# GRU products of four of six steps written as pairs of 64-row products, with three changes of order around them

## The chip, the cores and the metric

The kernel runs on one core of a Trainium2 chip. The metric is the device time of one execution in microseconds, median of three runs. Engines are called by the profile's names: PE multiplies matrices (PEld is its loading of weights), DVE does elementwise work, ACT activations, POOL further elementwise work, SP issues DMAs.

## The reference, cut to what matters

A decoder layer on x of 4 x 1024 tokens of 256 features: a gated recurrence with layer norms, then three rounds of slot attention over 64 context rows, ending each in a GRU, then a routed expert layer. The change lies in the middle part:

```python
for _ in range(3):
    sn = rmsnorm(slots, slot_norm_w)
    scores = einsum('bkd,bmd->bkm', sn @ Wq.T, k_proj) * 256 ** -0.5
    attn = softmax(scores, axis=-2)
    attn = attn / (sum(attn, axis=-1, keepdims=True) + 1e-6)
    updates = einsum('bkm,bmd->bkd', attn, v_proj)
    xr, xz, xn = split(updates @ wih.T + bih, 3)
    hr, hz, hn = split(slots @ whh.T + bhh, 3)
    r, z = sigmoid(xr + hr), sigmoid(xz + hz)
    n = tanh(xn + r * hn)
    slots = (1 - z) * n + z * slots
```

## The kernel before

Features lie on partitions and tokens on columns. Every round of attention treats the batches in two pairs, so there are six **steps** k = 0 to 5; steps 1 to 4 are one loop in the program of each engine, and they are the steps two to five of the change's name. A step has eight **units** q = 0 to 7: batch of the pair h = q // 4, half of its 1024 tokens j = (q // 2) % 2, half of the features c = q % 2. A unit is called (k, q); its number in a row is u = 8k + q.

A unit's products are those of `unit` (L1443). Weights and states are split in a high and a low part (`w_hh0`, `w_hh1`; `slots_hi`, `slots_lo`), so a hidden product of a gate is 2 halves of the features times 3 passes, 6 matmuls of 128 rows. The attention of a batch has 64 context rows: the tile `at` has its high part on one half of the partitions and its low part on the other, and the folded values (`v_ih_pair`: value projection times W_ih, high and low, each on both halves) are multiplied with it in 2 matmuls of 128 rows. The low half of the attention is thereby also multiplied with the low part of the values. A unit has 24 matmuls of 512 columns in this order: r (6 hidden, 2 of the attention), hn (6), xn (2), z (6 and 2). The banks of r and hn rotate among three, z has two, xn one, and the scores two.

The other engines follow unit by unit, each in its written order. ACT: `r_gate` (L762, sigmoid of r), `n_gate` (tanh), `z_gate`. DVE: `candidate` (L1856: `hidden_part` adds a bias to hn and multiplies by r, `input_part` adds xn), then `settle` (L1903: a multiplication, an addition, and after every second unit `high`, the cast to `slots_hi`). POOL: `difference` (L1014, state less candidate) between tanh and settling, `add_squares`, and `low` (for `slots_lo`).

The attention of step k+1 is made during step k. ACT squares the settled states of step k-1 (`squares`, L783), POOL adds them, PE takes means (`mean_squares`, L1341, inside unit 2), ACT makes roots (`rms`), PE the scores (`scores`, L1350, between units 2 and 3), DVE the maximum (`tops`), ACT `exponentials` after r of unit 4, DVE `weights`, PE `sums` in unit 5, ACT `normaliser` (L753: table load, Ln, Exp, table load) after r of unit 6, DVE `attention` (L1826) and `spread_attention` (L1832: a cast to `at`, and the remainder). `spread_attention(k+1, 0)` serves units (k+1, 0) to (k+1, 3), and the one for h = 1 follows in step k+1.

The matmuls wait for what frees their banks and for their inputs: r of a unit for `t_dve` (hn read two units before), hn for `r_act` (the sigmoid of the unit before), xn for `t2_dve` (`input_part` of the unit before), z for `z_act`, and the first attention product of each h for `at_lo`. The loop on PE reads:

```python
unit(k, 0)
unit(k, 1)
unit(k, 2, {"HN": lambda: mean_squares(k + 1)})
scores(k + 1)
unit(k, 3)
unit(k, 4)
unit(k, 5, {"XN": lambda: sums(k + 1)})
unit(k, 6)
```

## Time and profile before

| | |
|---|---|
| median of 3 runs (lowest to highest) | 550.38 us (549.33 to 550.53) |
| the profiled execution | 551.15 us |
| its span, from the first to the last instruction | 549.4 us |
| PE busy | 504.2 us (92%) |
| DVE, ACT, POOL busy | 435.6 (79%), 340.0 (62%), 240.8 us (44%) |
| matmuls of `unit` (L1459) | 1128, 34% of the chain that ended last |
| from unit (1, 0) to the end of unit (4, 6) | 204.9 to 409.9 us of the span |

The page's busy times are shares of the whole span. The steps that the change touches are read as stretches: the chain that ended last shows which engine sets the time there, the timeline shows in brackets how long an engine stood idle before an instruction and for whom.

### The profile page before, as it was taken

How to read it: one execution, taken by the hardware profiler on the slowest of the kernel's cores; microseconds unless marked ns; L12 is line 12 of the kernel's file. 1: busy time of each engine (PE TensorE's matmuls, PEld its weight loads, DVE VectorE, ACT ScalarE, POOL GpSimd, SP SyncE). 2: the span in 40 equal slices, each digit the busy share in tenths (PEclk: the TensorE clock that was granted, in tenths of full speed). 3: DMA queues.
4: the chain of work that ended last, by engine and by line, in shares of the span. 5: the costliest groups of instructions: out<-in, count | busy, mean ns of one | idle time of the engine just before them, and what ended most of it. 6: DMA issues, size and time to landing. Idle time of an engine off the chain costs nothing.

```text
span 549.4 us, 7254 instructions
## 1 busy us (share of the span) xinstructions
PE 504.2 (92%) x2154; PEld 362.0 (66%) x2154; DVE 435.6 (79%) x794; ACT 340.0 (62%) x600; POOL 240.8 (44%) x209
## 2 busy tenths in 40 slices
PE   6999996959779998899999999999999999979993
PEld 2466552725557686488858876886787788867672
DVE  2899999998799477999966986898579667868783
ACT  3656549784598484567456846766565676547443
POOL 0122030200123255655934674555435266647776
PEclk9999999878889999999999999999999999989997
DMA  8965395560521032000000000001011145255741
GB/s 292 315 211 78 105 164 147 138 136 1 76 78 61 17 78 78 0 2 0 2 1 0 1 0 1 1 2 62 24 68 40 39 171 204 88 165 164 223 148 65
DMA packets 34886, 47.32 MB, mean 86 GB/s; under 512 B 8062, under 2 KB 26623, under 8 KB 34561
## 3 DMA queue, kind: packets, MB, share of 16 engines
q1 hardware_dynamic: 27216, 34.25, 20.6%
q0 software_dynamic: 7632, 12.62, 9.4%
q8 instruction: 18, 0.29, 0.2%
q14 instruction: 20, 0.16, 0.1%
HBM read 25.70 MB, written 16.83 MB: 77 GB/s over the span
## 4 chain that ended last, share of the span: by engine, by line
PE 49%; issue 7%; DVE 6%; POOL 4%; ACT 3%; DMA 1%; SPq 1%; POOLq 0%; ACTq 0%; DVEq 0%
PE psum L1459 34%; PE psum L1552 6%; PE psum L1270 3%; PE psum L1523 2%; PE psum L1401 1%; PE psum L1347 1%; POOL gru L1022 1%; DVE gru L1874 1%; DMA gathered<-sorted_rows 1%; POOL sorted_rows L1052 1%; DVE gru L1847 1%; DVE gru L1854 1%; POOL slots_lo L1037 1%; PE psum L1359 1%; POOL out L1060 1%
## 5 line engine op out<-in xcount | busy, mean ns | idle before, releaser
L1459 PE MATMUL psum<-slots_hi,w_hh 128*128 128x512 f32 x560 | 180.1, 403 | 1.6 <-ACT gru L767 1.6
L1459 PEld LDWEIGHTS psum<-slots_hi,w_hh 128*128 128x128 f32 x560 | 104.0, 190 | 28.3 <-issue 4.2
L1022 POOL TENSOR_TENSOR gru<-slots_full,gru 128x512 f32<-128x512 f32 x43 | 65.8, 1529 | 108.2 <-ACT gru L773 108.1
L1459 PE MATMUL psum<-slots_lo,w_hh 128*128 128x512 f32 x280 | 111.6, 399 | 0.0
L1459 PE MATMUL psum<-at,v_ih_pair 128*128 128x512 f32 x288 | 92.4, 406 | 4.5 <-DVE at L1753 3.1
L773 ACT ACTIVATE gru<-gru,vec 128x512 f32<-128x512 f32 x48 | 34.6, 722 | 59.6 <-DVE gru L1854 59.5
L1459 PEld LDWEIGHTS psum<-at,v_ih_pair 128*128 128x128 f32 x288 | 54.2, 192 | 21.3 <-DVE at L1753 3.4
L1155 PE MATMUL psum<-early_hi,w_in 128*128 128x512 f32 x128 | 58.4, 616 | 5.0 <-DMA early_hi<-in_xT 5.0
L1847 DVE SCALAR_TENSOR_TENSOR gru<-psum,vec,gru 128x512 f32<-128x512 f32 x48 | 35.9, 748 | 32.9 <-PE psum L1459 26.8
L1459 PEld LDWEIGHTS psum<-slots_lo,w_hh 128*128 128x128 f32 x280 | 53.0, 189 | 12.7
L1874 DVE TENSOR_TENSOR gru<-gru 128x512 f32<-128x512 f32 x47 | 43.6, 929 | 8.6 <-POOL gru L1022 7.5
L1155 PEld LDWEIGHTS psum<-early_hi,w_in 128*128 128x128 f32 x128 | 25.2, 198 | 35.7 <-issue 34.3
L1037 POOL TENSOR_TENSOR slots_lo<-slots_full,slots_hi 128x512 fp32r<-128x512 f32 x32 | 47.1, 1472 | 0.6 <-DVE slots_hi L1900 0.6
L1876 DVE TENSOR_TENSOR slots_full<-gru 128x512 f32<-128x512 f32 x47 | 44.5, 947 | 1.6
L767 ACT ACTIVATE gru<-psum,brz 128x512 f32<-128x512 f32 x48 | 32.6, 679 | 21.2 <-PE psum L1459 21.2
L1552 PE MATMUL psum<-slots_full,w_tile 128*128 x156 | 43.3, 400 | 1.1 <-issue 0.4
L1060 POOL DMA_INDIRECT out<-out_tile,out_index x39 | 37.9, 972 | 12.6 <-issue 8.8
L1052 POOL DMA_INDIRECT sorted_rows<-row_block,dest x32 | 33.8, 1056 | 20.0 <-DVE dest L1962 8.6
L1031 POOL TENSOR_TENSOR ss_block<-sq_block 128x512 f32<-128x512 f32 x16 | 22.3, 1392 | 40.8 <-ACT sq_block L788 37.3
L1854 DVE TENSOR_TENSOR gru<-psum,gru 128x512 f32<-128x512 f32 x48 | 33.2, 692 | 6.5 <-PE psum L1459 5.0
L780 ACT ACTIVATE gru<-psum,brz 128x512 f32<-128x512 f32 x48 | 32.5, 677 | 0.9 <-PE psum L1459 0.6
L1552 PEld LDWEIGHTS psum<-slots_full,w_tile 128*128 128x128 f32 x156 | 26.5, 189 | 8.8 <-issue 5.4
(249 smaller groups left out, 855.0 us busy)
## 6 DMA issues: line engine op xcount, KB each, us to landing
gathered<-sorted_rows SPq DMA_DIRECT2D x39, 129.0 KB, 2.3
x_scratch<-slots_full SPq DMA_DIRECT2D x8, 512.0 KB, 3.0
x_block<-x_scratch SPq DMA_DIRECT2D x8, 512.0 KB, 3.9
early_hi<-in_xT SPq DMA_DIRECT2D x3, 1024.0 KB, 5.3
v_ih_pair<-value_part SPq DMA_DIRECT2D x32, 96.0 KB, 2.2
x_tm<-in_x SPq DMA_DIRECT2D x4, 512.0 KB, 6.9
x_tm<-ln_b POOLq DMA_DIRECT2D x4, 512.0 KB, 6.0
slots_full<-expert_plus SPq DMA_DIRECT2D x1, 2048.0 KB, 9.7
```

Of the source, the lines that this page charges most:

```text
L773: act.activation(X(u), X(u), ACT.Tanh, bias=col(c, V_BIH + 2)).then_inc(n_act, 1)
L1022: pool.tensor_tensor(DF(u), full[:, c, seq(k, h), blk(j)], X(u), ALU.subtract).then_inc(d_pool, 1)
L1037: last = pool.tensor_tensor(slots[1][:, c, b, blk(j)], full[:, c, b, blk(j)], slots[0][:, c, b, blk(j)].bitcast(F32), ALU.subtract)
L1052: pool.indirect_dma_start(rows[:], bass.IndirectOffsetOnAxis(dest[:, n:n + 1], 0), rowb[:, row_slot(n), :], None, bounds_check=E * REGION - 1,
L1060: pool.indirect_dma_start(out[:], bass.IndirectOffsetOnAxis(oidx[:, g % 4, t:t + 1], 0), og[:, i % (4 * TG), :], None, bounds_check=TOK - ...
L1155: last = pe.matmul(psum[:, bank + j, :], wi[:, k, at_col:at_col + P], xF[b % 2][:, k, cols_of(j)], start=k == 0, stop=k == C - 1)
L1459: last = pe.matmul(psum[:, bank, :], w, d, start=start and i == 0, stop=stop and i == len(pairs) - 1, skip_group_check=begun or late)
L1552: last = pe.matmul(expert_out(i), wT[:, i % TG, c, :], ew[:, c, bass.ds(off, D)], start=c == 0, stop=c == C - 1)
L1847: dve.scalar_tensor_tensor(out=X(u), in0=psum[:, hn_bank(u), :], scalar=col(c, V_BHH + 2), in1=X(u), op0=ALU.add, op1=ALU.mult).then_inc(t ...
L1854: dve.tensor_tensor(X(u), psum[:, XN_B, :], X(u), ALU.add).then_inc(t2_dve, 1)
L1874: dve.tensor_tensor(Z(u), Z(u), DF(u), ALU.mult).then_inc(e_dve, 1)
L1876: dve.tensor_tensor(full[:, c, seq(k, h), blk(j)], X(u), Z(u), ALU.add).then_inc(s_dve, 1)
```

## The change

**Pairs.** In the units from (1, 1) to (4, 6), 30 in all, `split_unit` takes the place of `unit`. Each matmul of 128 rows becomes one on rows 0 to 63 ("low") and one on rows 64 to 127 ("high"). Both add into the same bank, the high ones after the low ones of that bank are done (semaphore `low_rows`). `both` issues a low product of one gate next to a high product of another: r low with what is left of the unit before (xn high, z high), hn low with r high, z low with hn high. So hn's high part ends with the unit, and xn and z of a unit end some ten pairs into the next one.

**A product less.** Low attention times low values is left out: of a gate's 4 half products of the attention 3 are issued. The third needs the high attention on one given half of the partitions, so SP copies `at`'s high part (64 partitions by 1024 columns) to the other half, into `at_x` (in the program's rows `value_parts`), one DMA for each h of a step (`copy_attention`, which waits for both token halves). The first pair of unit (k, 1) waits for the copy of h = 0, unit (k, 4) for that of h = 1. A unit has 22 or 23 pairs in turn.

**Order.** `mean_squares`, `scores` and `sums` move to places inside units 2, 3 and 6, after nine or ten pairs (in step 1 `mean_squares` comes after 15). On ACT `r_gate` of units 1, 3, 5 and 7 goes ahead of `squares`. On DVE `attention` and `spread_attention` for h = 0 are cut by token halves (`first_of_pair`); the first half goes ahead of `settle(k, 5)`, the second behind `candidate(k, 7)`; `candidate`s of units 1 to 3 go ahead of `lows`, `second_of_pair` and `tops`. Semaphores are merged to make room for two new ones.

```diff
+                    low, high = both(one[0:2], x_before)
+                    if x_before:
+                        high.then_inc(xn_mm, 1)
+                        pe.wait_ge(low_rows, 4 * n_split - 4)
+                    low, high = both(one[2:], z_before[0:4])
...
+                        low, high = both(update(r, 0, lo, 1), z_before[4:6])
+                        low.then_inc(low_rows, 1)
+                        pe.wait_ge(r_act, u)
+                        low, high = both(two[0:max(nz - 6, 1)], z_before[6:])
...
+                        pe.wait_ge(low_rows, 4 * n_split - 3)
+                        n = len(two)
+                        low, high = both(two, r_hi[0:n])
+                        low.then_inc(low_rows, 1)
+                        highs = r_hi[n:]
...
+                    pe.wait_ge(t2_dve, u)
+                    low, high = both(update(XN_B, 2, lo, 0), highs[0:1])
...
+                    z_lo = hidden(z, 1, lo) + update(z, 1, lo, u % 2)
+                    n = len(highs)
+                    low, high = both(z_lo[0:n], highs)
...
+                        high.then_inc(r_mm, 1)
+                        pe.wait_ge(low_rows, 4 * n_split - 2)
+                        low, high = both(z_lo[n:], hn_hi)
+                        high.then_inc(hn_mm, 1)
...
+                    return update(XN_B, 2, hi, 1), hidden(z, 1, hi) + update(z, 1, hi, 1 - u % 2)
...
+                def copy_attention(k, h):
+
+                    n = 2 * k + h
+                    sp.wait_ge(at_hi, at_made(k, h, J - 1))
+                    if n > 2:
+                        sp.wait_ge(at_copied, 16 * (n - 2))
+                    if k > 1:
+                        sp.wait_ge(z_mm, U * (n - 1))
+                    sp.dma_start(at_x[half(1 - h), :].bitcast(F32),
+                                 at[n % 3][half(h), :].bitcast(F32)).then_inc(at_copied, 16)
...
+                    rest = split_unit(k, 1, rest)
+                    rest = split_unit(k, 2, rest, {"XN" if k == 1 else "R": lambda: mean_squares(k + 1)})
+                    rest = split_unit(k, 3, rest, {"R": lambda: scores(k + 1)})
+                    rest = split_unit(k, 4, rest)
+                    rest = split_unit(k, 5, rest)
+                    rest = split_unit(k, 6, rest, {"R": lambda: sums(k + 1)}, last=k + 2 == PAIRS)
```

The same on the engines. PE, the start of unit (1, 6) before: r takes 8 matmuls of 128 rows, then hn begins (L1459 is the one line of `unit`'s matmuls; the number is that of the buffer).

```order
L1459 MATMUL psum<-slots_hi,w_hh0 128x512 [waits t_dve]
L1459 MATMUL psum<-slots_hi,w_hh1 128x512
L1459 MATMUL psum<-slots_lo,w_hh0 128x512
L1459 MATMUL psum<-slots_hi,w_hh0 128x512
L1459 MATMUL psum<-slots_hi,w_hh1 128x512
L1459 MATMUL psum<-slots_lo,w_hh0 128x512
L1459 MATMUL psum<-at0,v_ih_pair1 128x512 x2
L1459 MATMUL psum<-slots_hi,w_hh0 128x512 [waits r_act]
L1459 MATMUL psum<-slots_hi,w_hh1 128x512
```

PE, the start of unit (1, 6) now: L1542 issues the low rows, L1545 the high rows, so r's low rows stand in turn with xn and z of unit (1, 5).

```order
L1542 MATMUL psum<-slots_hi,w_hh0 128x512 [waits low_rows,t_dve]
L1545 MATMUL psum<-at0,v_ih_pair1 128x512
L1542 MATMUL psum<-slots_hi,w_hh1 128x512
L1545 MATMUL psum<-at0,v_ih_pair1 128x512
L1542 MATMUL psum<-slots_lo,w_hh0 128x512 [waits low_rows]
L1545 MATMUL psum<-slots_hi,w_hh0 128x512
L1542 MATMUL psum<-slots_hi,w_hh0 128x512
L1545 MATMUL psum<-slots_hi,w_hh1 128x512
L1542 MATMUL psum<-slots_hi,w_hh1 128x512
L1545 MATMUL psum<-slots_lo,w_hh0 128x512
L1542 MATMUL psum<-slots_lo,w_hh0 128x512
L1545 MATMUL psum<-slots_hi,w_hh0 128x512
```

The 8 products of r are no longer a block of their own; two gates of the unit before end among them.

DVE before, from `candidate(3, 6)` on (L1847 and L1854; `settle` is L1874, L1876 and the cast L1900), with the attention for step 4 in L1828 to L1840:

```order
L1847 SCALAR_TENSOR_TENSOR gru<-psum,vec,gru 128x512
L1854 TENSOR_TENSOR gru<-psum,gru 128x512
L1874 TENSOR_TENSOR gru<-gru 128x512
L1876 TENSOR_TENSOR slots_full<-gru 128x512
L1900 CAST slots_hi<-slots_full 128x2x512
L1828 SCALAR_TENSOR_TENSOR sc<-sc,small,inv 128x1024
L1838 CAST at<-sc 64x1024
L1840 TENSOR_TENSOR at<-sc,at 64x1024
L1847 SCALAR_TENSOR_TENSOR gru<-psum,vec,gru 128x512
L1854 TENSOR_TENSOR gru<-psum,gru 128x512
```

DVE now, the same place in the program (`candidate` L2024 and L2031, `settle` L2051 to L2077, attention L1997 to L2010):

```order
L2024 SCALAR_TENSOR_TENSOR gru<-psum,vec,gru 128x512
L2031 TENSOR_TENSOR gru<-psum,gru 128x512
L1997 SCALAR_TENSOR_TENSOR sc<-sc,small,inv 128x512
L2008 CAST at<-sc 64x512
L2010 TENSOR_TENSOR at<-sc,at 64x512
L2051 TENSOR_TENSOR gru<-gru 128x512
L2053 TENSOR_TENSOR slots_full<-gru 128x512
L2077 CAST slots_hi<-slots_full 128x2x512
L2024 SCALAR_TENSOR_TENSOR gru<-psum,vec,gru 128x512
L2031 TENSOR_TENSOR gru<-psum,gru 128x512
L1997 SCALAR_TENSOR_TENSOR sc<-sc,small,inv 128x512
L2008 CAST at<-sc 64x512
```

The attention's first half of 512 columns moved ahead of `settle(3, 5)`, its second half behind `candidate(3, 7)`.

ACT before, in a step, from the normaliser's second table load on (L773 tanh and L780 z of unit 6, L788 squares, L767 r of unit 7):

```order
L760 ACT_TABLE_LOAD
L773 ACTIVATE gru<-gru,vec 128x512
L780 ACTIVATE gru<-psum,brz 128x512
L788 ACTIVATE sq_block<-slots_full 128x1024
L767 ACTIVATE gru<-psum,brz 128x512
L773 ACTIVATE gru<-gru,vec 128x512
```

ACT now, the same place (L801, L808, L795, L816):

```order
L788 ACT_TABLE_LOAD
L801 ACTIVATE gru<-gru,vec 128x512
L808 ACTIVATE gru<-psum,brz 128x512
L795 ACTIVATE gru<-psum,brz 128x512
L816 ACTIVATE sq_block<-slots_full 128x1024
L801 ACTIVATE gru<-gru,vec 128x512
```

r of unit 7 and the squares changed places.

## Rows read from the trace of the kernel before

**Rows 1.** Windows: stretch, us; busy us of PE, PEld, DVE, ACT, POOL; clock; DMA.

```profile
204.89:231.52 26.63, 23.00 (x97) 14.93 (x95) 22.38 (x24) 13.79 (x18) 15.38 (x14) 1.00 0.23 80
283.13:334.74 51.61, 51.52 (x222) 38.40 (x221) 41.40 (x47) 32.78 (x41) 29.52 (x21) 1.00 0.00 1
```

**Rows 2.** Chain that ended last, one step: start us, us, what.

```profile
299.23 27.44 PE psum L1459 x118
...
331.06 0.09 issue
```

**Rows 3.** Timeline, PE, step 1: start, us, instruction, idle before it and releaser.

```profile
219.70 0.74 PE L1459 MATMUL psum<-slots_hi,w_hh 128*128 128x512 f32 x2 [1.59 <-ACT gru L767]
...
221.58 1.94 PE L1347 MATMUL psum<-ss_block,mean_f 128*64 128x512 f32 x8 [0.21 <-POOL ss_block L1031]
...
227.94 3.65 PE L1270 MATMUL psum<-slots_full,fold 128*64 128x512 f32 x16 [1.83 <-ACT inv L742]
```

**Rows 4.** Timeline, ACT and DVE, the same place.

```profile
218.02 1.06 ACT L788 ACTIVATE sq_block<-slots_full 128x1024 f32<-128x1024 f32 x1 [3.44 <-DVE slots_full L1876]
...
218.64 3.44 DVE L1697 TENSOR_TENSOR slots_lo<-slots_full,slots_hi 128x512 fp32r<-128x512 f32 x2
```

**Rows 5.** Groups on PE by shape: count, busy us, mean ns, idle before.

```profile
L1155 PE MATMUL psum<-early_hi,w_in 128*128 128x512 f32 x128 | 58.4, 616 | 5.0 <-DMA early_hi<-in_xT 5.0
...
L1287 PE MATMUL psum<-stack_f,ones_halves 64*64 64x512 f32 x8 | 1.9, 602 | 0.0
```

**Rows 6.** Weight loads of three lines: ns min/median/max, first and last start, shape.

```profile
L1459 PEld LDWEIGHTS psum<-slots_hi,w_hh x560: 186/188/337, 148.2 to 478.3; 128*128 128x128 f32 x187
...
L1347 PEld LDWEIGHTS psum<-ss_block,mean_f x32: 132/136/137, 221.6 to 379.1; 128*64 128x64 f32 x32
...
L1287 PEld LDWEIGHTS psum<-stack_f,ones_halves x8: 129/133/133, 136.6 to 137.6; 64*64 64x64 f32 x8
```

**Rows 7.** Timeline, PE, from products of 128 columns to products of 64.

```profile
326.27 0.40 PE L1459 MATMUL psum<-slots_lo,w_hh 128*128 128x512 f32 x1
326.60 1.94 PE L1347 MATMUL psum<-ss_block,mean_f 128*64 128x512 f32 x8
```

**Rows 8.** Timeline, ACT, r of unit (3, 6) and the normaliser for step 4.

```profile
303.08 0.68 ACT L767 ACTIVATE gru<-psum,brz 128x512 f32<-128x512 f32 x1
...
306.22 1.06 ACT L759 ACTIVATE inv<-inv 128x1024 f32<-128x1024 f32 x1
307.31 1.28 ACT L760 ACT_TABLE_LOAD   x1
```

**Rows 9.** Timeline, DVE, settling, candidate and attention around the same place.

```profile
301.77 1.17 DVE L1874 TENSOR_TENSOR gru<-gru 128x512 f32<-128x512 f32 x1
302.97 1.67 DVE L1876 TENSOR_TENSOR slots_full<-gru 128x512 f32<-128x512 f32 x1
304.56 0.74 DVE L1847 SCALAR_TENSOR_TENSOR gru<-psum,vec,gru 128x512 f32<-128x512 f32 x1
305.34 0.69 DVE L1854 TENSOR_TENSOR gru<-psum,gru 128x512 f32<-128x512 f32 x1
305.94 0.68 DVE L1874 TENSOR_TENSOR gru<-gru 128x512 f32<-128x512 f32 x1
...
307.38 0.69 DVE L1900 CAST slots_hi<-slots_full 128x1024 fp32r<-128x1024 f32 x1
307.99 1.28 DVE L1828 SCALAR_TENSOR_TENSOR sc<-sc,small,inv 128x1024 f32<-128x1024 f32 x1
...
310.03 2.21 DVE L1840 TENSOR_TENSOR at<-sc,at 64x1024 fp32r<-64x1024 f32 x1
...
330.75 1.22 DVE L1840 TENSOR_TENSOR at<-sc,at 64x1024 fp32r<-64x1024 f32 x1
```

**Rows 10.** DMA issues: count, KB each, median us from issue to landing.

```profile
v_ih_pair<-value_part SPq DMA_DIRECT2D x32, 96.0 KB, 2.2
...
x_scratch<-slots_full SPq DMA_DIRECT2D x8, 512.0 KB, 3.0
```

More of the change, by code:

```diff
@@ L321, in block_of, with at_made @@
             return i // J, blk(i % J)
+        def at_made(k, h, j):
+            n = 2 * k + h
+            return n + 1 + n // 2 - (1 if k > 0 and h == 0 and j == 0 else 0)
         def pair_banks(t):
@@ L1506, in unit, with both @@
                     run(Z_B + u % 2, update(1), start=False).then_inc(z_mm, 1)
+                def both(lows, highs):
+                    low = high = None
+                    for i in range(max(len(lows), len(highs))):
+                        if i < len(lows):
+                            bank, w, d, start = lows[i]
+                            low = pe.matmul(psum[:, bank, :], w, d, start=start, stop=False, skip_group_check=True)
+                        if i < len(highs):
+                            bank, w, d, start = highs[i]
+                            high = pe.matmul(psum[:, bank, :], w, d, start=start, stop=True, skip_group_check=True)
+                    return low, high
@@ L1564, in _ @@
                 unit(0, 7)
+                rest = [], []
                 for k in range(1, LAST):
[L1566 to L1573 removed]
+                    if k == 1:
+                        unit(k, 0)
+                    else:
+                        rest = split_unit(k, 0, rest)
+                    rest = split_unit(k, 1, rest)
[4 more added lines that the diff above has]
+                    rest = split_unit(k, 6, rest, {"R": lambda: sums(k + 1)}, last=k + 2 == PAIRS)
                     if k + 2 < PAIRS:
[L1575 removed]
+                        rest = split_unit(k, 7, rest)
                 def tiles_after(*these):
@@ L2151, in _ @@
                 settle(0, 5)
-                attention(1)
-                spread_attention(1, 0)
+                first_of_pair(1, 0)
+                first_of_pair(1, 1)
                 candidate(0, 7)
```

195 lines of the change are left out of this document (149 added, 46 removed).

## The prediction

> **What bounds the kernel now.** I read the page's shares first, then the chain that ended last, then single steps. In the chain, from 231 us to 409 us every piece is PE's, but for a wait of 0.09 us a step [rows 2]. A step of 51.61 us has PE busy for 51.52, DVE for 41.40, ACT for 32.78 and POOL for 29.52, at a granted clock of 1.00, which is 2.4 GHz [rows 1]. So in steps 2 to 4 a product less on PE is time won, until another engine's chain becomes longer than PE's. 118 matmuls in a row took 27.44 us [rows 2]: one costs 0.2325 us, called a slot below. Step 1 is different: PE is busy for 23.00 of 26.63 us [rows 1] and stands idle three times, 1.59 us for a sigmoid, 0.21 for POOL's sums of squares, 1.83 for the roots [rows 3].
>
> **The slots.** 30 units of 24 matmuls are 720 slots. A split unit has 22 pairs (u even) or 23 (u odd). Counted in the program, units (1, 1) to (4, 6) have 675 slots with at least one half product, 18 of them with one alone (9 at the start, 9 at the end of the series), and 10 whole matmuls in unit (4, 6): 685. If a pair costs what a whole matmul costs, 35 slots go: 35 x 0.2325 = **8.1 us less**.
>
> That a pair costs a slot is no row of this trace; the nearest are products on a quarter of the array. Eight records of 64 rows by 64 columns took 1.9 us, 0.24 us each, where records of the full array and the same 512 columns took 58.4 / 128 = 0.456 us [rows 5]. Two ran at a time. They used other rows and other columns of the array; the new pairs share the columns. I take one slot, with 0.006 us either way: 4 pairs in 1.9 us are 0.475 us a pair against 0.456, of which a part is the ends of a short run. Where PE sets the time (685 less the 156 slots under the chain below) that is 3 us either way.
>
> The Trainium skill says in "TensorE: Matmul & The Clock Gate", LDWEIGHTS (loading the stationary operand), that a load of 32 rows takes as long as one of 128, because its time goes by columns. Two rows bear it out: 64 columns took 133 ns with 64 rows and 136 with 128 [rows 6]. By the page a pair then has two loads of full length, which speaks against the change; the sum above needs them to overlap, and the price of the other case is rival C.
>
> **Changes of form.** Where products of 128 columns give way to ones of 64, the next product started 0.33 us after the last, a slot and 0.10 [rows 7]. `mean_squares` and `scores` have such changes before and after. `sums` was of the same form as its neighbours and is now a whole product among pairs: two more a step, 4 x 2 x 0.10 = **0.8 us more**. Bounds: 0 and 1.6.
>
> **New waits of PE on itself.** High products wait for the low ones of their bank. A matmul takes 0.40 us from start to end [rows 7]; where only two slots (0.465) lie between the last low one and the first high one (units 0 and 4; in 2 and 6 other products stand between), about 0.08 is lost with the wake-up: 7 x 0.08 = **0.5 us more**, from 0 to 2.
>
> **Step 1.** r of unit (1, 1) was late because ACT had `squares` ahead of it and stood 3.44 us for DVE [rows 4]. With r ahead, the 1.59 goes. `scores` comes ten slots (2.3 us) into unit 3 instead of before it, which covers the 1.83. What is late next is xn of unit (1, 2): `candidate(1, 1)` can start on DVE only where the two `lows` of 3.44 us now start, at 218.6 [rows 4], and is done 1.5 us later [rows 9], while PE, with unit (1, 0) from 204.9 [rows 1] and so unit (1, 1) from 210.5, is there after 37 slots at 219.1. That keeps 1.2 with the wake-up, and the sums of squares some 0.3: of 3.63 us **2.1 less**. Bounds: 0.5 and 3.6.
>
> **Step boundaries: the copy.** This is the term that decides. In the old order `at` was ready a little before its first use. Now unit (k, 1) of steps 2, 3 and 4 starts with a wait for the copy of `at`, and that copy needs both token halves of the attention, the second of which stands behind `candidate(k-1, 7)`. The chain, from the end of r's products in unit 6:
>
> - product to its end 0.40 [rows 7], then sigmoid, table load, Ln, Exp: 303.08 to 307.28, 4.20 [rows 8]. Together 4.6.
> - DVE, first half: half of 1.28, of the cast of 0.69 and of the remainder of 1.22: 1.6. `settle(5)`: 0.68 twice and the cast of 0.69, 2.05. `candidate(7)`: 0.74 and 0.69. Second half to the cast: 1.0. With gaps of 0.2: 6.3 [rows 9]. Beside POOL's work the same operations took 1.17 and 1.67 instead of 0.68, and 2.21 instead of 1.22 [rows 9]; tanh of unit 6 comes 2.0 us after Exp (the second table load of 1.28 [rows 8] and itself), so POOL's difference falls on `settle(5)`. I add 0.5, by the first of these: 6.8. Were all of them stretched, it would be 9.8.
> - the DMA of 256 KB: between 2.2 (96 KB) and 3.0 (512 KB) [rows 10], say 2.5, and 0.2 for SP and PE to wake.
>
> That is 14.1 us. PE has work for 7 slots of unit 6, 23 of unit 7 and 22 of unit 0, 52 x 0.2325 = 12.1. PE waits 2.0 us, a part of it already in unit 0, where xn waits for `candidate(7)`. Three boundaries: **6.0 us more**. Bounds: all alone, DMA 2.2: 13.3, so 1.2 each, 3.6; all stretched, DMA 3.0: 17.6, so 5.5 each, 16.5. Behind the wait stands all of PE; SP has nothing else in its queue then, and the loads of x1 that follow its last copy wait for `mean_squares(5)` as before.
>
> The scores' wait of 0.09 a step, 0.3 in all, goes [rows 2]: from r's products in unit 2 to Ln's end ACT needs 0.4 and 3.1 us [rows 8], and PE has 17 slots, 4.0 us. The new order of `squares` leaves `mean_squares` about as much room as the boundary's delay takes from it: 0, at most 1 a step. The attention's halves cost DVE two instructions more a step, in gaps it has (10 us a step idle [rows 1]). After unit (4, 6) step 5 has whole units; it moves as it stands.
>
> **Sum.** -8.1 + 0.8 + 0.5 - 2.1 + 6.0 - 0.3 = -3.2 us. The profiled execution took 551.15 us, its span 549.4; the median of the runs is 0.8 under it. The difference goes against the median: 550.4 - 3.2 = **547.2 us**.
>
> **The rivals.**
> A. *The copy comes in time.* If the chain is no longer than 12.1 us, the boundaries cost nothing and the sum is -9.2: 541.2 us. For it: DVE idles a fifth of a step [rows 1], and the first half's operations can overlap in part, as 305.94 to 307.99 shows three operations in 2.05 us [rows 9]. Against: even without POOL beside it the rows add up to 13.3.
> B. *The copy takes PE's place* (slower). If the boundary costs more than 9.2 / 3 = 3.1 us, the gain is gone. At 4.5 each it is -9.2 + 13.5: 554.7 us. For it: remainder and settling have rows of twice the length [rows 9], and POOL's difference and sums fall there. Against: it takes more than four of these operations stretched, each time.
> C. *The halves don't run side by side* (slower). If the two loads of a pair follow each other, a slot is 2 x 0.188 [rows 6] = 0.376, 685 x 0.144 = 98 us more, and PE then covers the copy: about 640 us; if the products do, 685 x 0.2325 = 159 us more, about 700. For it: no row has two products on the same columns and other rows. Against: [rows 5]. The page's rule on loads gives this result only if loads queue, and eight loads of 0.133 fit into the 1.9 us of [rows 5] either way, so the trace doesn't decide it.
>
> **How the numbers follow.** Forecast (boundary 1.2 to 3.1, about 544 to 550) 0.45; A 0.22; B 0.26; C 0.07. A measurement of this kernel tells 0.2% (1.1 us) from no change. Faster by more than that: 0.36 of the forecast and A, 0.58. Within: 0.06 of the forecast and 0.05 of B, 0.11. Slower: 0.03 of the forecast, 0.21 of B, and C, 0.31. The range runs from A's time to B's with boundaries of 4.9: 541 to 556. It leaves out C, the longest boundaries, and A with a cheaper pair.
>
> **What would show it.** Right: pairs start 0.23 us apart at a clock of 1.00; step 2 takes about 51 us, of which PE idles some 2 us, in units 0 and 1, for DVE and for the copy; in step 1 no wait for `r_act`. Wrong in the slot: half products 0.19 us or more apart, in turn. Wrong at the boundary: no idle time before the first pair of unit (k, 1), or more than 3 us. Wrong elsewhere: PE waiting for `ssum_done`, for scores' roots or for `t2_dve` in the middle of a step.

## The result and the profile after

| | before | after |
|---|---|---|
| median (lowest to highest), four runs each, side by side | 550.45 us (549.33 to 550.91) | 562.02 us (560.28 to 562.62) |
| ratio of the two, 95% interval | | 1.021 (1.019 to 1.023) |
| span of the profiled execution | 549.4 us | 560.5 us |
| a step (from the scores of step 2 to those of step 3) | 51.61 us | 53.32 us |

The change made the kernel 2.1% slower; 547.2 was forecast, and the time lies outside the range of 541 to 556. The page after, PE, DVE and the granted clock in 40 slices:

```profile
PE 502.4 (90%) x2776; PEld 359.3 (64%) x2776; DVE 448.0 (80%) x809; ACT 341.7 (61%) x600; POOL 241.2 (43%) x209
...
PEclk9999999969889999999899999999998999989997
...
PE 37%; issue 11%; DVE 9%; POOL 7%; ACT 5%; DMA 1%; SPq 1%; POOLq 0%; DVEq 0%; ACTq 0%
```

The last line is the chain that ended last: PE has 37% of it, where it had 49%. In the steps DVE, ACT, POOL and "issue" (time for which the profile names no releaser) now have links in it, where before there was PE alone [rows 2]. The stretches from scores to scores, columns as in [rows 1]:

```profile
232.04:285.98 53.94, 51.37 (x390) 38.42 (x388) 47.47 (x55) 34.02 (x42) 31.59 (x22) 0.97 0.07 11
286.02:339.34 53.32, 49.92 (x391) 36.49 (x389) 45.03 (x50) 33.12 (x40) 29.81 (x21) 1.00 0.05 11
339.34:392.70 53.36, 49.97 (x392) 36.64 (x390) 44.34 (x49) 33.13 (x40) 29.84 (x21) 1.00 0.11 31
```

PE is busy for 1.6 us less a step than before (49.9 against 51.52), so the products did become cheaper; it is idle for 3.4 where it was idle for 0.1. One start of pairs, PE and its weight loads (start us, us, instruction):

```profile
296.23 0.39 PE L1545 MATMUL psum<-at,v_ih_pair 64*128 64x512 f32 x1
296.23 0.62 PE L1542 MATMUL psum<-slots_hi,w_hh 64*128 64x512 f32 x2
296.46 0.39 PE L1545 MATMUL psum<-at,v_ih_pair 64*128 64x512 f32 x1
...
296.23 0.18 PEld L1545 LDWEIGHTS psum<-at,v_ih_pair 64*128 64x128 f32 x1
296.23 0.18 PEld L1542 LDWEIGHTS psum<-slots_hi,w_hh 64*128 64x128 f32 x1
```

Low and high product start together, the next pair 0.23 us later, and both loads run at once. PE's waits around the boundary to step 3 and at the start of step 5 (in brackets the idle time before, and who ended it):

```profile
315.77 0.50 PE L1542 MATMUL psum<-at,v_ih_pair 64*128 64x512 f32 x1 [0.69 <-DVE gru L2031]
319.79 0.47 PE L1542 MATMUL psum<-slots_hi,w_hh 64*128 64x512 f32 x1 [1.90 <-issue]
328.34 1.94 PE L1375 MATMUL psum<-ss_block,mean_f 128*64 128x512 f32 x8 [0.81 <-POOL ss_block L1059]
...
420.75 1.21 PE L1429 MATMUL psum<-eye_and_gate,slots_full 128*128 128x137 f32 x8 [0.67 <-DVE eye_and_gate L2089]
429.74 0.71 PE L1429 MATMUL psum<-eye_and_gate,slots_full 128*128 128x137 f32 x4 [4.05 <-ACT row_block L824]
```

The first is xn of unit (3, 0), the second the first pair of unit (3, 1), which waits for the copy, the third `mean_squares` in unit (3, 2). The last two are the routing's tiles in unit (5, 0). (By this count the unit of [rows 8] is (2, 6), the sixth unit before the boundary to step 3. The text ahead of the prediction numbers it, and the normaliser with it, one step too high; nothing in the sums hangs on that.)

What led to the three waits is one chain over four engines. ACT, DVE and POOL, from r of unit (2, 6) on (L795 sigmoid, L787 the normaliser's Exp, L1997 and L2008 attention, L2051 and L2053 settling, L2031 end of a candidate, L1050 POOL's difference, L1059 its sum of squares; rows between them are left out):

```profile
305.01 0.68 ACT L795 ACTIVATE gru<-psum,brz 128x512 f32<-128x512 f32 x1
308.15 1.06 ACT L787 ACTIVATE inv<-inv 128x1024 f32<-128x1024 f32 x1
309.25 0.75 DVE L1997 SCALAR_TENSOR_TENSOR sc<-sc,small,inv 128x512 f32<-128x512 f32 x1 [1.28 <-ACT inv L787]
311.33 1.73 POOL L1050 TENSOR_TENSOR gru<-slots_full,gru 128x512 f32<-128x512 f32 x1 [2.53 <-ACT gru L801]
311.94 1.67 DVE L2053 TENSOR_TENSOR slots_full<-gru 128x512 f32<-128x512 f32 x1
315.03 0.69 DVE L2031 TENSOR_TENSOR gru<-psum,gru 128x512 f32<-128x512 f32 x1
316.41 0.42 DVE L2008 CAST at<-sc 64x512 fp32r<-64x512 f32 x1
317.63 1.76 POOL L1059 TENSOR_TENSOR ss_block<-sq_block 128x512 f32<-128x512 f32 x1 [4.57 <-DVE at L2010]
322.38 1.76 DVE L2051 TENSOR_TENSOR gru<-gru 128x512 f32<-128x512 f32 x1 [1.05 <-POOL gru L1050]
327.01 1.27 POOL L1059 TENSOR_TENSOR ss_block<-sq_block 128x512 f32<-128x512 f32 x1 [1.72 <-ACT sq_block L816]
```

From the sigmoid at 305.01 to `mean_squares` at 328.34 it took 23.3 us. Before, the same two points lay 303.08 [rows 8] and 326.60 [rows 7], 23.5 us apart, and PE worked all of that time. After, PE has 23.3 less its waits there, 19.5 us of work. The chain was there before the change too, but out of sight. POOL's last sum of squares ahead of `mean_squares` in the kernel before:

```profile
321.00 1.69 POOL L1031 TENSOR_TENSOR ss_block<-sq_block 128x512 f32<-128x512 f32 x1
```

It ended 19.6 us after the sigmoid of r, 3.9 us before PE came to `mean_squares`; after the change it ends 23.3 us after the sigmoid, and PE waits for it. This is the reading that the experiments test:

**Theory C.** A step is a closed loop of two parts: from `mean_squares` to r of unit 6, PE's work alone (30.0 us after, 28.1 before), and from r of unit 6 to the next `mean_squares`, the longer of PE's work and a chain over ACT, DVE and POOL. In pair units PE's work in the second part became 4.0 us shorter; the chain did not (it is 3.7 us longer). **Rivals**: each wait is a cost of its own, and the copy the main one (A); the new order on DVE is the cause (D), not the pairs.

### The profile page after: what moved, and what is told of

Its sections match the earlier page's. It is cut to its first block, busy times and chain, and to the rows that moved or that the text cites. A ratio compares the mean times of both kernels' runs of the same rounds, so it can differ in the third digit from the quotient of the medians.

```text
span 560.5 us, 8564 instructions
## 1 busy us (share of the span) xinstructions
PE 502.4 (90%) x2776; PEld 359.3 (64%) x2776; DVE 448.0 (80%) x809; ACT 341.7 (61%) x600; POOL 241.2 (43%) x209
## 4 chain that ended last, share of the span: by engine, by line
PE 37%; issue 11%; DVE 9%; POOL 7%; ACT 5%; DMA 1%; SPq 1%; POOLq 0%; DVEq 0%; ACTq 0%
PE psum L1542 10%; PE psum L1487 7%; PE psum L1718 6%; PE psum L1545 5%; PE psum L1298 3%; POOL gru L1050 2%; POOL slots_lo L1065 2%; PE psum L1429 2%; PE psum L1689 1%; POOL ss_block L1059 1%; PE psum L1375 1%; DVE gru L2024 1%; DVE gru L2031 1%; DVE slots_full L2053 1%; DVE at L2008 1%
## 5 line engine op out<-in xcount | busy, mean ns | idle before, releaser
L1542 PE MATMUL psum<-slots_hi,w_hh 64*128 64x512 f32 x356 | 115.1, 400 | 5.7 <-issue 5.7
L1545 PE MATMUL psum<-slots_hi,w_hh 64*128 64x512 f32 x356 | 114.4, 401 | 0.0
L1050 POOL TENSOR_TENSOR gru<-slots_full,gru 128x512 f32<-128x512 f32 x43 | 64.0, 1488 | 94.0 <-ACT gru L801 94.0
L1542 PEld LDWEIGHTS psum<-slots_hi,w_hh 64*128 64x128 f32 x356 | 66.0, 186 | 21.6 <-issue 12.0
L1542 PE MATMUL psum<-slots_lo,w_hh 64*128 64x512 f32 x178 | 70.9, 398 | 0.0
L1545 PE MATMUL psum<-slots_lo,w_hh 64*128 64x512 f32 x178 | 70.8, 398 | 0.0
L801 ACT ACTIVATE gru<-gru,vec 128x512 f32<-128x512 f32 x48 | 34.7, 723 | 54.8 <-DVE gru L2031 54.7
L1545 PEld LDWEIGHTS psum<-slots_hi,w_hh 64*128 64x128 f32 x356 | 64.7, 186 | 5.2
L1487 PE MATMUL psum<-slots_hi,w_hh 128*128 128x512 f32 x200 | 67.0, 417 | 0.0
L2024 DVE SCALAR_TENSOR_TENSOR gru<-psum,vec,gru 128x512 f32<-128x512 f32 x48 | 35.8, 745 | 29.6 <-PE psum L1545 18.5
L2053 DVE TENSOR_TENSOR slots_full<-gru 128x512 f32<-128x512 f32 x47 | 53.0, 1128 | 1.6
L795 ACT ACTIVATE gru<-psum,brz 128x512 f32<-128x512 f32 x48 | 32.8, 683 | 34.7 <-PE psum L1545 26.2
L2051 DVE TENSOR_TENSOR gru<-gru 128x512 f32<-128x512 f32 x47 | 45.5, 968 | 9.7 <-POOL gru L1050 8.6
L1065 POOL TENSOR_TENSOR slots_lo<-slots_full,slots_hi 128x512 fp32r<-128x512 f32 x32 | 49.0, 1532 | 0.6 <-DVE slots_hi L2077 0.6
L1059 POOL TENSOR_TENSOR ss_block<-sq_block 128x512 f32<-128x512 f32 x16 | 22.0, 1377 | 62.4 <-ACT sq_block L816 48.7
L1542 PE MATMUL psum<-at,v_ih_pair 64*128 64x512 f32 x111 | 40.8, 401 | 3.1 <-DVE gru L2031 3.1
L1487 PEld LDWEIGHTS psum<-slots_hi,w_hh 128*128 128x128 f32 x200 | 37.3, 196 | 8.1 <-issue 1.0
```

Of the source, the lines that this page charges most:

```text
L801: act.activation(X(u), X(u), ACT.Tanh, bias=col(c, V_BIH + 2)).then_inc(n_act, 1)
L1050: pool.tensor_tensor(DF(u), full[:, c, seq(k, h), blk(j)], X(u), ALU.subtract).then_inc(d_pool, 1)
L1065: last = pool.tensor_tensor(slots[1][:, c, b, blk(j)], full[:, c, b, blk(j)], slots[0][:, c, b, blk(j)].bitcast(F32), ALU.subtract)
L1487: last = pe.matmul(psum[:, bank, :], w, d, start=start and i == 0, stop=stop and i == len(pairs) - 1, skip_group_check=begun or late)
L1542: low = pe.matmul(psum[:, bank, :], w, d, start=start, stop=False, skip_group_check=True)
L1545: high = pe.matmul(psum[:, bank, :], w, d, start=start, stop=True, skip_group_check=True)
```

## The experiments

Times are medians, with the ratio to runs of the kernel before on the same chip. The first expectations call theory C "B", and those on what the pairs do to the room in it "W".

### The copy in halves

```diff
-                    sp.wait_ge(at_hi, at_made(k, h, J - 1))
+                    for j in range(J if h == 0 else 1):
+                        sp.wait_ge(at_hi, at_made(k, h, j if h == 0 else J - 1))
...
-                    if q == 1:
-                        pe.wait_ge(at_copied, 16 * (2 * k + h - 1))
+                    if q == 1 or q == J + 1:
+                        pe.wait_ge(at_copied, 16 * copied(k, 0, j))
...
```

> The copy of the attention for h = 0 goes in two DMAs, one per token half; the first pair of unit (k, 1) waits for the first half alone, and unit (k, 3) for the second. Theory A (the copy is a wait of its own): the wait of 1.9 us before unit (k, 1) goes three times, with the restart some 6 us in all, 562.0 - 5.7 to 6.2 = about 556 us. Theory B (one chain bounds the boundary: second half of the attention, POOL's sums, difference and settling of unit 7, squares, sums of squares, mean_squares): the wait before unit (k, 1) goes too, but PE then waits some 2 us more for ss_block in unit (k, 2); the time stays within 1 us of 562, or 1.4 us less if the stretch at half clock after the copy of step 2 does not come back.

Measured: 565.49 us, ratio 1.026 (1.023 to 1.030), slower than the change. PE's wait for `mean_squares`, and the clock (column after POOL) behind it:

```profile
328.32 3.50 PE L1381 MATMUL psum<-ss_block,mean_f 128*64 128x512 f32 x8 [2.46 <-POOL ss_block L1065]
...
328.30:331.70 3.40, 3.38 (x8) 0.77 (x8) 3.34 (x3) 0.98 (x2) 3.40 (x3) 0.53 0.00 0
```

The copy's wait went, and `mean_squares` of step 3 started at 328.32, where it had started at 328.34. Theory A falls: 1.9 us taken from one wait came back in the next. The time is 2.5 us above what theory C (there B) allowed, and that is the clock: after this wait it was granted at half for some 3 us, and the eight products took 3.50 us in place of 1.94. This came at all three boundaries; in the change it came at one.

### POOL's wait, alone and with the copy in halves

```diff
-                        pool.wait_ge(at_lo, at_made(k + 1, 0, J - 1))
+                        pool.wait_ge(at_lo, at_made(k + 1, 0, 0))
```

> POOL's third sum of squares of a step waits for the first half of the attention alone, not for the second; everything else is as in the changed kernel. Theory B: POOL is free some 3 us earlier for the difference of unit 7, settling and the sums of squares are earlier, and the wait of 0.8 us before mean_squares goes in steps 3 and 4 while the copy's wait of 1.9 stays: about 560.4 us. Against it: POOL then runs beside candidate(k, 7) and the second half on DVE and stretches them by up to 1 us each; then the copy's wait grows to 3 or 4 us, and the time is 562 to 567.

> Both edits: the copy in halves and POOL's wait on the first half alone. Theory A (waits that add up): what the two single edits gave, added. Theory B (one chain behind two waits): more than the sum of the two, since the copy in halves alone only moves the wait to mean_squares: 562.0 - 3 x 2.05 (copy) - 2 x 0.8 (sums of squares) = about 554.5 us, if POOL does not stretch DVE's work.

Measured: 568.36 us, 1.032 (1.027 to 1.036), and 565.78 us, 1.027 (1.024 to 1.031). First PE and DVE with POOL's wait alone, then PE with both edits:

```profile
322.23 0.76 PE L1542 MATMUL psum<-slots_hi,w_hh 64*128 64x512 f32 x1 [3.13 <-issue]
...
317.86 1.40 DVE L2008 CAST at<-sc 64x512 fp32r<-64x512 f32 x1
319.30 1.64 DVE L2010 TENSOR_TENSOR at<-sc,at 64x512 fp32r<-64x512 f32 x1
```

```profile
323.70 0.50 PE L1548 MATMUL psum<-at,v_ih_pair 64*128 64x512 f32 x1 [2.48 <-DVE gru L2037]
```

POOL's sums now ran beside the second half of the attention and stretched its cast from 0.42 to 1.40 us and the remainder from 0.69 to 1.64; the copy's wait grew to 3.1. With both edits neither the copy nor the sums of squares were waited for, and the wait stood at xn of unit (3, 1), for `candidate(3, 0)`. Alone, the edit is slower than either forecast for it. The forecast of 554.5 for the pair of edits missed: I had taken the links out that PE named and left DVE's row of work as long as it was, or longer. In both runs PE also ran at half clock behind the wait at all three boundaries (0.50 from 324.6 to 327.8 us with both edits).

### Settling ahead of the attention

```diff
                     candidate(k, 6)
-                    first_of_pair(k + 1, 0)
                     settle(k, 5)
+                    first_of_pair(k + 1, 0)
```

> On DVE settle(k, 5) goes back ahead of the first half of the attention, as it stood before the change; nothing else. DVE stands idle 1.3 us there for the normaliser, and settling takes 2 to 3 us. Theory (the boundary hangs on DVE's chain after the normaliser): that chain is 1.3 to 2.2 us shorter, so xn's wait of 0.7 in unit 0 goes and the copy's wait shrinks by what is left, each boundary gives 1.3 to 2.0 and step 5 as much: 562.0 - 4 x 1.7 = about 555 us. Rival (settle(k, 5) is stretched by POOL beside it and ends no earlier than the attention could start): within 1 us of 562.

Measured: 558.56 us, 1.016 (1.013 to 1.019). Settling fills DVE's idle time; r to `mean_squares` is 22.8 us instead of 23.3, a step 52.8. The direction is the theory's, the size half of it: half of what settling took ahead of the attention pushed the attention back (it starts 5.7 us after r instead of 4.2). By the profile the boundary to step 2 gave 3.0 us, 1.6 of them the half clock that did not come there, the other two 0.5 each, and the start of step 5, for which as much was expected, nothing: PE's wait for `row_block` is 4.11 us. The profiled execution was the fastest of this kernel, 2.1 us below the median.

### The new orders with whole products

PE's loop is that of the kernel before, the copy is left out, and ACT, DVE and POOL keep the orders of the change.

```diff
-                    rest = split_unit(k, 1, rest)
-                    rest = split_unit(k, 2, rest, {"XN" if k == 1 else "R": lambda: mean_squares(k + 1)})
-                    rest = split_unit(k, 3, rest, {"R": lambda: scores(k + 1)})
...
+                    unit(k, 1)
+                    unit(k, 2, {"HN": lambda: mean_squares(k + 1)})
+                    scores(k + 1)
+                    unit(k, 3)
...
```

> The changed kernel's orders on DVE, ACT and POOL, but whole products of 128 rows on PE in the old order of units, without the copy. Theory W (a pair unit leaves the other engines less room: hn's and xn's high rows end with the unit or two pairs into the next one, and the next xn comes ten pairs in, so that DVE has some 2 us for a candidate where whole units left it over 5): with whole units the new orders cost nothing at the boundaries; steps take 51.6 us with no wait in units 0 to 2, step 1 gains its 2 us, and only the start of step 5 stays late by some 4: 550.4 - 2 + 4 = about 552.5 us. Rival D (the new order of DVE makes the boundary late by itself): waits of 2 to 3 us stay at each boundary, 558 us or more.

Measured: 557.08 us, 1.013 (1.010 to 1.015). A step by the windows, POOL's last sum of squares in it, and PE's wait in step 5:

```profile
281.76:333.36 51.60, 51.51 (x222) 38.40 (x220) 44.69 (x51) 32.62 (x41) 30.90 (x20) 1.00 0.00 1
...
324.24 1.29 POOL L1041 TENSOR_TENSOR ss_block<-sq_block 128x512 f32<-128x512 f32 x1 [1.72 <-ACT sq_block L798]
...
423.54 1.25 PE L1411 MATMUL psum<-eye_and_gate,slots_full 128*128 128x137 f32 x4 [4.07 <-ACT row_block L806]
```

Steps 2 to 4 took 51.60 us with PE busy all the time, as before the change: with whole units the new orders cost the boundaries no time, so D alone falls there. But they use up the room: POOL's last sum ends 23.4 us after r of unit (2, 6), where it was 19.6, and 0.25 us before `mean_squares`, where it was 3.9. Whole products still cover that chain; the pairs, with 19.5 us of work, do not. Step 5 has the wait of 4 us all the same, so that part belongs to the order. The time is 4.5 us above what was expected: step 1 waited 2 us for the sums of squares and ran on at half clock, and so did PE in step 5 (0.50 from 422.5 to 429.0 us), which lost more than its 4.4.

### The pairs with the old orders

ACT's and DVE's orders as before the change; in the last turn and in all others both halves of the attention stand together.

```diff
-                    first_of_pair(k + 1, 0)
                     settle(k, 5)
+                    first_of_pair(k + 1, 0)
...
+                    first_of_pair(k + 1, 1)
                     candidate(k, 7)
-                    first_of_pair(k + 1, 1)
...
-                    r_gate(k, 1)
                     squares(k - 1, 3)
+                    r_gate(k, 1)
...
```

> Pairs and copy as in the changed kernel, but the orders on DVE and ACT as before the change (squares ahead of r, candidates behind tops and lows, both halves of the attention behind settle(k, 5) and ahead of candidate(k, 7)). Theory W (the pairs take the room away): no wait for the copy, but xn of unit (k, 0) waits 2 to 3 us for candidate(k-1, 7), which stands behind the whole attention, and step 1 has its waits again; the start of step 5 is better than in the changed kernel: 555 to 561 us. Rival (the orders are to blame, the pairs gain their 8 us): 543 to 547 us.

Measured: 555.57 us, 1.009 (1.007 to 1.011). PE's waits of one step:

```profile
304.60 0.49 PE L1542 MATMUL psum<-slots_hi,w_hh 64*128 64x512 f32 x1 [0.91 <-ACT gru L795]
319.42 0.50 PE L1542 MATMUL psum<-at,v_ih_pair 64*128 64x512 f32 x1 [1.22 <-DVE gru L2031]
```

A step takes 52.05 us: still above 51.6, but the wait for the copy and that for the sums of squares are gone, and r to `mean_squares` is 20.85 us. POOL's last sum ends 20.2 us after r, and PE does not wait for it; what is left are the waits of 0.91 for r and 1.22 for xn. So both are true: the pairs take the room away, and the new orders make the chain longer.

### The last turn alone

```diff
-                    first_of_pair(k + 1, 0)
+                    if later:
+                        first_of_pair(k + 1, 0)
                     settle(k, 5)
                     if not later:
+                        first_of_pair(k + 1, 0)
                         gate_centre()
+                        first_of_pair(k + 1, 1)
                     candidate(k, 7)
-                    first_of_pair(k + 1, 1)
+                    if later:
+                        first_of_pair(k + 1, 1)
```

> Only in the last turn of the loop, on DVE: settle(4, 5), then both halves of the attention, with the gate's centre between them as before the change, then candidate(4, 7). Theory S (the wait of 4.4 us for row_block in unit (5, 0) is the attention's long way on DVE, 12.7 us from the normaliser's Exp to the end of the remainder, where it was 8): the wait shrinks to 1 or less, candidate(4, 7) comes 2 us later and xn of unit (5, 0) takes up to 1 of that back: 558 to 559.5 us. Rival (DVE is stretched there by POOL beside it, whatever the order: one cast took 2.74 us): within 1 us of 562.

Measured: 557.19 us, 1.013 (1.010 to 1.015), 4.8 us less than the change. PE's wait for `row_block`, the rows that ACT writes for the routing:

```profile
423.56 0.71 PE L1429 MATMUL psum<-eye_and_gate,slots_full 128*128 128x137 f32 x4 [0.90 <-ACT row_block L824]
```

Theory S holds: 4.05 became 0.90. The loss in step 5 was the attention's way on DVE in the last turn. In the change, ACT's rows wait for the remainder of this cast, which POOL had stretched:

```profile
424.92 2.74 DVE L2008 CAST at<-sc 64x1024 fp32r<-64x1024 f32 x1
427.70 1.22 DVE L2010 TENSOR_TENSOR at<-sc,at 64x1024 fp32r<-64x1024 f32 x1
```

### Settling first, the last turn, and POOL's difference earlier

The two edits of those names, and on POOL, for the third sum of a step (m = 2):

```diff
                         difference(k, 2 * m + 2)
-                        if later:
+                        if later and m < 2:
                             add_squares(k, m)
                             low(k, m, 0)
                         difference(k, 2 * m + 3)
                         if later:
+                            if m == 2:
+                                add_squares(k, m)
+                                low(k, m, 0)
                             low(k, m, 1)
```

> Pairs, with settle(k, 5) ahead of the attention in all turns, the last turn as in the run that changes it alone, and POOL's difference of unit 7 ahead of its third sum of squares. If the boundary is one chain over DVE and POOL that ends in mean_squares, each link that is taken out gives its length: 558.6 - 4 (step 5) - 3 x 1 (POOL) = about 551.5 us. If POOL's difference beside the second half of the attention stretches DVE instead, the copy comes later by up to 1 us a step and the time is 554.5 to 557.

Measured: 551.18 us, 1.002 (1.001 to 1.003). The time is the expected one, but not by the expected terms; it is 7.4 below the run with settling alone, of which the last turn gives 4.8. POOL's edit, for which 1 us a step was expected, gave 0.3 by the profile: r to `mean_squares` went from 22.8 to 22.5 us. So that each link gives its length is not shown here. The 1.8 us that are left are in no wait of the two profiles, of which the one with settling alone is 2.1 below its median.

### Both halves of the attention together, then a second bank

The first kernel is the change with settling first, then `first_of_pair` twice, then `candidate(k, 7)`, in all turns. The second adds:

```diff
+        def xn_bank(k, q):
+            return S_B + 1 if q == 0 and 1 < k < LAST else XN_B
...
-                    pe.wait_ge(t2_dve, u)
-                    low, high = both(update(XN_B, 2, lo, 0), highs[0:1])
+                    if xn_bank(k, q) == XN_B:
+                        pe.wait_ge(t2_dve, u - (q == 1 and k > 1))
+                    low, high = both(update(xn_bank(k, q), 2, lo, 0), highs[0:1])
...
```

> The changed kernel with one place on DVE as before the change, in every turn: settle(k, 5), then both halves of the attention (the gate's centre between them in the last turn), then candidate(k, 7). ACT's order and the candidates ahead of lows, tops and the second spreading stay new. Theory C (a step is PE's work from mean_squares to r of unit 6, 30.0 us, and behind it the chain from r to the next mean_squares, in which PE has 19.5 us of work; the halves apart make that chain 23.3 us, together they made it 20.9 in the run of the pairs in the old order): steps of 30.0 + 20.9 = 50.9 us, no wait for the copy or for mean_squares, 1.4 us for xn in unit (k, 0), and the start of step 5 without its 4.4: about 548.5 us, below the kernel before. Rival (the new order of the candidates is a part of the long chain): steps of 52 us or more, 552 to 556 us.

> The same, and xn of unit (k, 0) in steps 2 to 4 adds into a bank of the scores, which stands empty between the normaliser and mean_squares, so that it need not wait until candidate(k-1, 7) has read xn's one bank. Theory W (the wait left there is for the bank alone): steps of 49.6 us, three times 1.3 us less than the run without it, about 544.5 us. Rival (DVE is the limit at the boundary, not the bank): the wait moves to xn of unit (k, 1) or to mean_squares, and the time is within 1 us of the run without it.

Measured: 550.16 us, 1.000 (0.998 to 1.001), and 548.52 us, 0.996 (0.994 to 0.998). PE's waits at the boundary to step 3 in the first, then in the second:

```profile
309.88 0.50 PE L1542 MATMUL psum<-at,v_ih_pair 64*128 64x512 f32 x1 [0.56 <-DVE at L2010]
313.34 0.49 PE L1542 MATMUL psum<-at,v_ih_pair 64*128 64x512 f32 x1 [1.25 <-DVE gru L2031]
```

```profile
309.60 0.49 PE L1547 MATMUL psum<-at,v_ih_pair 64*128 64x512 f32 x1 [0.57 <-DVE at L2016]
...
322.04 1.94 PE L1380 MATMUL psum<-ss_block,mean_f 128*64 128x512 f32 x8 [0.55 <-POOL ss_block L1062]
```

r to `mean_squares` is 21.7 us in the first and 21.1 in the second, a step 51.7 and 51.1. The first lies between its two forecasts: the halves apart made the chain longer, but together they are 21.7 us and not 20.9, so other parts of the new orders count too. In the second the bank's wait of 1.25 is gone, and 0.6 of it are won; the rest came back before `mean_squares`. There too both theories hold in part.

### The squares later, alone and together with all of it

In the change, `mean_squares` of steps 2 to 4 moves by some six pairs:

```diff
-                    rest = split_unit(k, 2, rest, {"XN" if k == 1 else "R": lambda: mean_squares(k + 1)})
+                    rest = split_unit(k, 2, rest, {"XN": lambda: mean_squares(k + 1)})
```

> The changed kernel, only mean_squares of steps 2 to 4 some six pairs later in unit 2, as it stands in step 1. Theory C: the wait of 0.8 to 0.9 us before it goes in steps 3 and 4, and the scores, which come 1.4 us closer behind it, still find their roots: 562.0 - 1.8 = about 560.3 us. Rival (the room for Ln is then too short, 17 pairs or 4.0 us against 0.4 and 3.1 and the way there): a wait before the scores of 0.5 to 1 in place of it, 562 us.

Measured: 560.99 us, 1.020 (1.016 to 1.023). The wait before `mean_squares` went and none came before the scores; of the 1.8 us some went to more time at half clock after the copy's waits. The same edit, the copy in halves and the cast of `settle(k, 5)` behind the attention, on top of the second bank:

> The run with the extra bank for xn (548.5 us), and three edits at the waits that are left in its steps: the cast of settle(k, 5) behind the attention (0.6 us of the wait for the first half in unit (k, 0)), the copy for h = 0 in halves (the wait before unit (k, 1): 1.1 in step 4, 0.35 in step 2), mean_squares some six pairs later (0.66 each in steps 2 and 3). Theory C (with the extra bank the chain is short enough that what is left adds up): 548.5 - 3 x 0.6 - 1.4 - 1.3 = about 544 us. Rival (the chain over DVE and POOL is at its end: a wait that goes comes back at the next place, as the copy in halves alone did): 547 to 549 us.

Measured: 545.36 us, 0.992 (0.990 to 0.994). From `mean_squares` to `mean_squares`:

```profile
271.62:321.68 50.06, 49.98 (x391) 36.03 (x389) 45.12 (x51) 32.69 (x41) 30.24 (x21) 1.00 0.05 11
```

PE is busy for 49.98 of 50.06 us: the loop is closed by PE alone again, and the copy in halves, which lost 3.5 us by itself, now costs nothing. This kernel is 0.8% faster than the one before; what each of the three edits gave of it, no run shows. The chain in the runs, for the boundary to step 3 (each from the start of ACT's sigmoid of r of unit (2, 6) and the starts of the `mean_squares` around it; the last column is the end of the last sum of squares on POOL, counted from the same sigmoid):

| kernel | `mean_squares` to r of unit 6 | r to `mean_squares` | together | r to POOL's last sum |
|---|---|---|---|---|
| before | 28.1 | 23.5 | 51.6 | 19.6 |
| new orders, whole products | 28.0 | 23.6 | 51.6 | 23.4 |
| the change | 30.0 | 23.3 | 53.3 | 23.3 |
| copy in halves | 31.6 | 23.3 | 55.0 | 23.3 |
| POOL's wait | 30.0 | 25.0 | 55.0 | 24.6 |
| settling first | 30.0 | 22.8 | 52.8 | 22.7 |
| old orders, pairs | 31.2 | 20.9 | 52.1 | 20.2 |
| attention together | 30.0 | 21.7 | 51.7 | 21.3 |
| and a second bank | 30.0 | 21.1 | 51.1 | 21.0 |
| all together | 28.6 | 21.5 | 50.1 | 20.8 |

The 31.6 holds the half clock, the 31.2 the wait for r. The last row's parts are cut six pairs later.

## Why the prediction was wrong, step by step

| term, us | predicted | measured |
|---|---|---|
| slots | -8.1 | -7.7 |
| changes of form, waits of PE on itself | +1.3 | +3.0 |
| step 1 | -2.1 | -2.0 |
| scores' wait | -0.3 | in the second row |
| boundaries: xn of unit 0, copy | +6.0 | +8.7 |
| waits before `mean_squares` in steps 3 and 4 | 0 | +1.8 |
| half clock at one boundary | not in the sum | +1.6 |
| start of step 5 | 0 | +5.2 |
| sum | -3.2 | +10.6, and the span grew by 11.1 |

The measured column is worked out from the starts of PE's products, a wait being what lies above a slot. Of the span's 11.1, 0.6 lies ahead of the changed steps.

**The slots: right.** In long runs pairs stood 0.233 us apart at a clock of 1.00. Rival C falls: the loads of both halves run at once, 0.18 us each. The page "TensorE: Matmul & The Clock Gate" of the Trainium skill, LDWEIGHTS, says that a load's time goes by its columns; the trace agrees (186 ns for 64 rows, 186 to 188 for 128 [rows 6]). That rule, weighed as speaking against the change, did not bear: the two loads of a pair, on different rows, did not queue.

**Changes of form: right in kind, too few.** A start after a wait, after a change of form or after a product of the low rows that the high ones need is about 0.1 later than a slot. There are 35 such starts among the units' products where there were nine, and `sums` among pairs took 0.3 a step.

**Step 1: right.** The wait for `r_act` and that of the scores went; 1.2 stayed at xn of unit (1, 2), as forecast, and 0.65 before `mean_squares`, where 0.3 was.

**The boundary: the chain was right, its end was not.** From r of unit 6 to the first pair of unit (3, 1) the text had 14.1 us; it was 319.79 less 305.01, 14.8, the copy taking 2.9 by the DMA rows where 2.5 stood. The first step that failed is "The new order of `squares` leaves `mean_squares` about as much room as the boundary's delay takes from it: 0, at most 1 a step". I followed the chain to the first point where PE waits and stopped there. It runs on, through POOL's wait for the second half, the settling of unit 7 and its squares, to `mean_squares`. Before, POOL's last sum ended 19.6 us after r and PE came to it after 23.5, so there were 3.9 us of room. The new orders take 3.7 of them, and the pairs shorten PE's 23.5 to 19.5. The orders alone still fit (0.25 us left with whole products), both together make PE wait for 3.8 us a step (23.3 less 19.5), at whichever place it comes to first. That the wait left at `mean_squares` is 0.9 in steps 3 and 4, inside the "at most 1", is due to the waits before it: with the copy in halves it is 2.5. Where PE's 23.5 began and ended was in [rows 7] and [rows 8], and PE's work in the new form could be counted as the first part's was; where POOL's last sum ended stood in the trace (321.00 and 1.69), but in no term.

**What the form of a unit does to the others.** I counted slots saved and not where in the unit its results come. By a count of the program r ends in the 16th or 17th slot of its unit where it was the 8th, and `mean_squares` comes after the 10th where it was after the 14th. From the one to the other PE has some 84 slots and had 102: 18 x 0.233 = 4.2 us, where the runs have 4.0. xn is complete two pairs into the next unit, and DVE must have read it by that unit's 15th slot: 12 slots or 2.8 us, where it had 22 or 5.1. (The expectation of the whole products put the next xn at ten pairs; it is the fifteenth.) The run with whole products shows no wait at the boundaries with the same orders, and the one with the second bank that xn's bank was 0.6 us of a step.

**Step 5: "it moves as it stands" was wrong.** This is the second step that failed. The sum left out that in the last turn settling, the gate's centre and `candidate(4, 7)` stand between the two halves, with ACT's rows behind both: 5.2 us, the largest single miss of the sum, of which the run with the last turn alone gave back 4.8. Some 4.5 of it stand before `row_block`'s products, the rest behind them, where PE ran at half clock for some 3 us. It was the same edit whose cost I worked out for three boundaries; I did not follow it to the fourth, where another consumer waits.

**Rival B** named the right side but the wrong mechanism: the boundary at 2.9 each would alone have left a gain of half a microsecond in the sum, and taking the copy's wait away won nothing. The range missed because the start of step 5 stood at nothing without a bound and the half clock was not in it: without these two, 6.8 us, the measured time would by the table be about 555 us, inside its upper end.

## What to carry to other kernels

Where PE is the busiest engine by a hair, look for the loop that closes over the other engines, count PE's work between its two ends, and look how long before PE the chain ends there: work taken out of PE is won only as far as that room goes, and an order that lengthens the chain spends the same room. Two edits that each fit into it need not fit together. When products are put in another form, note at which slot each result is ready and each bank is wanted, not only how many slots there are. An order changed inside a loop is costed once for every consumer, the last turn's too; and a wait taken out where PE shows it may only move, so the first edit to try here was the one that shortens the busiest row of work in the chain.

## What the runs showed of the hardware

**Two products of 64 rows cost what one of 128 costs**, 0.233 us a pair, loads included. Here the two always add into different banks; no run has them in one.

**The clock after a wait.** In the steps of the change PE ran at half clock once, after the wait at the boundary to step 2, and again behind the wait of 4.05 us in step 5:

```profile
266.00:267.00 1.00, 1.00 (x10) 0.90 (x10) 0.97 (x2) 0.00 (x0) 1.00 (x1) 1.00 0.07 16
267.00:268.00 1.00, 1.00 (x8) 0.87 (x7) 0.33 (x1) 0.64 (x1) 1.00 (x2) 0.58 0.00 0
268.00:269.00 1.00, 1.00 (x7) 0.90 (x6) 0.64 (x1) 0.08 (x1) 1.00 (x2) 0.50 0.00 0
...
431.00:434.00 3.00, 3.00 (x10) 2.56 (x9) 1.62 (x4) 2.34 (x7) 1.79 (x1) 0.50 0.00 0
```

Pairs stood 0.43 us apart in the first of the two. The same waits at the next two boundaries left it at 1.00, and in the run with the squares later the boundaries to steps 2 and 4 had it, that to step 3 not (0.57 from 371 to 375 us of that run). What decides between them stays open. Where it comes, a wait of 2 to 3 us costs some 1.6 more than itself, and in the run with POOL's wait more still (0.50 from 376.4 to 383.0 us); several runs are slower for it than their waits say.

**DVE beside POOL.** Settling took 0.69 us alone and 1.67 beside a POOL instruction of 1.7, a cast of 1024 columns 2.74. The Trainium skill's "SBUF — State Buffer", Summary: rules for kernel authors, says that a DVE instruction in a two-port mode, or one with two SBUF inputs beside one of GpSimd that reads SBUF, shares with GpSimd so that the second to issue waits for the first. The trace agrees for the settling, which has two inputs. The casts have one and are stretched too; whether they ran in the two-port mode, no run here shows. That POOL's wait for the attention protected DVE, and was not slack, was shown by taking it away: 6.3 us slower, a part of it the half clock at all three boundaries.
